# A sign-weight feed-forward and attention block on one core: layer 1's third copy of a running sum goes, its sum with the fifth product is written to that product's bank, and the queues are ordered anew

## What is computed

```python
xn = _layernorm(x, axis=-1)
# attention
q, k, v = einsum('bim,mhd->bhid', xn, wq / wk / wv);  q, k = rope(q), rope(k)
s = einsum('bhid,bhjd->bhij', q, k) / 128, masked causally
o = einsum('bhij,bhjd->bhid', softmax(s), v);  attn = einsum('bhij,hdm->bim', o, wo)
# feed-forward, w(k) = where(k, 1, -1)
h = s0 * concat([xn, -xn]) @ w(k0);  h = relu(h) * 2
h = s1 * h @ w(k1);                  h = relu(h) * 2
h = s2 * h @ w(k2)
out = x + attn + h
```

## Time and profile before

| | |
|---|---|
| median of the runs (lowest, highest) | 1728.72 us (1728.67, 1729.3) |
| the profiled execution's own time | 1728.13 us |
| its span, first to last instruction | 1726.3 us |
| PE busy / weight loads | 1713.5 us (99%) / 1202.2 us (70%) |
| ACT / DVE / POOL busy | 1467.6 (85%) / 1386.2 (80%) / 890.4 us (52%) |
| mean granted TensorE clock | 0.999 |

### The profile page before, as it was taken

How to read it: one execution, slowest core, us unless ns; L and a number is a source line. 1 busy time by engine, 2 the same in 40 slices (tenths; PEclk the granted TensorE clock), 3 DMA queues, 4 the chain that set the end, 5 groups by cost and what they waited for, 6 DMA issues and landing times.

```text
span 1726.3 us, 34270 instructions
## 1 busy us (share of the span) xinstructions
PE 1713.5 (99%) x12752; PEld 1202.2 (70%) x12752; DVE 1386.2 (80%) x3374; ACT 1467.6 (85%) x3229; POOL 890.4 (52%) x696
## 2 busy tenths in 40 slices
PE   8999999999999999999999999999999999999999
PEld 4567667677676776767667676676767767677677
DVE  8997887887878878688787877878788787886875
ACT  7898897888979889798897988979789797897984
POOL 7654655354654635556354563555635556354531
PEclk9999999999999999999999999999999999999999
DMA  5234434343434433444434343344433534353343
GB/s 177 56 72 85 93 60 93 68 90 64 76 81 65 98 60 71 86 72 83 68 62 86 74 81 68 68 85 70 92 56 82 79 61 93 58 94 71 62 81 68
DMA packets 454838, 134.08 MB, mean 78 GB/s; under 512 B 434704, under 2 KB 453648, under 8 KB 454672
## 3 DMA queue, kind: packets, MB, share of 16 engines
q1 hardware_dynamic: 454672, 131.90, 40.1%
HBM read 14.94 MB, written 8.39 MB: 14 GB/s over the span
## 4 chain that ended last, share of the span: by engine, by line
PE 95%; ACT 2%; DVE 2%; DMA 1%; SPq 0%; issue 0%; POOL 0%; DVEq 0%; ACTq 0%
PE bank L238 44%; PE bank L699 21%; PE bank L683 12%; PE bank L666 12%; PE bank L710 6%; DMA v<-in_wk 1%; ACT bank L427 1%; DVE pt L514 0%; ACT ph L431 0%; DMA xnat<-in_x 0%; DVE hb L549 0%; DVE ph L585 0%; SPq L282 0%; DVE wq L537 0%; ACT tb L409 0%
## 5 line engine op out<-in xcount | busy, mean ns | idle before, releaser
L351 POOL TENSOR_TENSOR tb<-tb,sin 128x512 f32<-128x512 f32 x256 | 324.7, 1273 | 445.4 <-ACT tb L410 442.7
L354 POOL TENSOR_TENSOR qk<-tb,qk 128x512 f16<-128x512 f32 x256 | 295.7, 1160 | 284.3 <-ACT qk L413 284.1
L699 PE MATMUL bank<-hb,wa 128*128 128x256 f16 x3360 | 391.3, 273 | 0.2 <-DVE ph L585 0.2
L699 PEld LDWEIGHTS bank<-hb,wa 128*128 128x128 fp8e5 x3360 | 327.3, 98 | 53.7 <-DVE ph L585 0.4
L427 ACT ACTIVATE bank<-bank,nm,sc 128x512 f32<-128x512 f32 (+3 forms) x512 | 301.3, 591 | 2.6
L585 DVE SCALAR_TENSOR_TENSOR ph<-bank,rk,ph 128x512 f16<-128x512 f32 (+3 forms) x512 | 254.1, 545 | 23.0 <-ACT ph L431 21.3
L575 DVE CUSTOM_DVE_ANT_0 bank<-bank,mask 128x512 f32<-128x512 f32 (+3 forms) x512 | 238.5, 518 | 20.4 <-PE bank L666 20.1
L557 DVE TENSOR_TENSOR bank<-bank,cos 128x512 f32<-128x512 f32 x256 | 176.7, 697 | 87.3 <-ACT tb L410 87.1
L683 PEld LDWEIGHTS bank<-pt,v 128*128 128x128 f16 x2304 | 203.7, 98 | 41.5 <-DMA pt<-ph 0.8
L431 ACT ACTIVATE ph<-bank,rk 128x512 f16<-128x512 f32 (+3 forms) x512 | 230.1, 541 | 2.4 <-DVE rk L582 1.4
L683 PE MATMUL bank<-pt,v 128*128 128x256 f16 (+1 forms) x2304 | 231.1, 255 | 0.0
(11 more groups left out here) (113 smaller groups left out, 2343.9 us busy)
## 6 DMA issues: line engine op xcount, KB each, us to landing
out<-xnat SPq DMA_DIRECT2D x32, 256.0 KB, 2.2
xnat<-in_x SPq DMA_DIRECT2D x15, 512.0 KB, 3.8
pt<-ph SPq DMA_TRANSPOSE x256, 4.3
o<-in_k SPq DMA_DIRECT2D x1, 1024.0 KB, 7.5
v<-in_wq SPq DMA_DIRECT2D x1, 1024.0 KB, 9.5
v<-in_wk SPq DMA_DIRECT2D x1, 1024.0 KB, 11.3
ph<-in_wv SPq DMA_DIRECT2D x1, 1024.0 KB, 13.5
o<-in_wo SPq DMA_DIRECT2D x1, 1024.0 KB, 10.9
```

What stands on the lines that cost most here:

```text
L351: pool.tensor_tensor(tb, tb, SIN[:], ALU.mult).then_inc(s_crossed, 1)
L354: pool.tensor_tensor(QK[:, g % 2, 2 * w + 1, :], TB[:, (2 * g + w) % TRING, :], QK[:, g % 2, 2 * w, :], ALU.subtract).then_inc(s_qk_lo, 1)
L699: mm = pe.matmul(ps[:, 256 * u:256 * u + 256], WA[:, w, k, (2 * j + u) * 128:(2 * j + u) * 128 + 128], HB[:, h, s, k, :], start=first and ...
```

## The change

For each j the third copy goes. `add_p5_to` reads the running sum's bank, adds S5, and writes the result into the bank of the fifth product, which `keep_p5` has read by then; product 4 accumulates on the running sum itself. The fifth product's bank is thus held until `h1_hi` and `h1_lo` have read it. The ACT queue loses 30 copies (90 to 60 instructions `bank<-bank` 128x512); every other kind of instruction keeps its count on every engine. All five orders are laid anew, from the start to the end, with another table ROTATION.

The new helper, the first line of the table, and `vector_program` in a repeated block:

```diff
+        def add_p5_to(dve, ps, dst):
+            dve.tensor_tensor(dst[:, :], ps[:, :], S5, ALU.add).then_inc(s_add, 1)
...
-            [0, 5, 1, 3, 4, 2, 6, 7],
+            [4, 6, 1, 3, 2, 0, 7, 5],
...
+                dve.wait_ge(s_prod, 14 * b - 16)
+                add_p5(dve, ps[3])
+                dve.wait_ge(s_h1_hi, 8 * b - 10)
+                h1_lo(dve, 1, 0, 1, ps[3])
+                dve.wait_ge(s_prod, 14 * b - 15)
+                add_p5_to(dve, ps[0], ps[4])
```

`scalar_program` loses the third copy there:

```diff
-                act.wait_ge(s_prod, 14 * b - 15)
-                act.wait_ge(s_rot, 16 * b - 1)
-                copy_sum(act, ps[5], ps[7])
```

At the start, `scalar_program` and then `vector_program`:

```diff
-            xT_first_hi(act, 0, BANK[0])
             xT_first_hi(act, 1, BANK[1])
-            act.wait_ge(s_k0, 2)
-            sign_k0(act, 0)
-            act.wait_ge(s_k0, 3)
-            sign_k0(act, 3)
             act.wait_ge(s_k_in[1], 16)
             convert_k1_act(act, 5)
+            xT_first_hi(act, 0, BANK[0])
...
-            dve.wait_ge(s_xT_hi, 1)
+            dve.wait_ge(s_xT_hi, 2)
             xT_first_lo(dve, 0, BANK[0])
-            dve.wait_ge(s_xT_hi, 2)
             xT_first_lo(dve, 1, BANK[1])
```

More of the change, by code:

```diff
@@ L1934, in scalar_program @@
+            h1_hi(act, 1, 1, 1, BANK[4])
+            xp_hi(act, 2)
+            act.wait_ge(s_PV, 11)
+            o_hi(act, 10, BANK[0])
             act.wait_ge(s_rot, 30)
@@ new lines, in tensor_program @@
+            pe.wait_ge(s_pt[0], 320)
+            pe.wait_ge(s_P_lo, 80)
+            values(pe, 18, BANK[6])
+            product(pe, 0, 2, range(8), BANK[5])
+            product(pe, 0, 3, range(8), BANK[3])
+            pe.wait_ge(s_o, 17)
+            qk(pe, 22, 1, BANK[2])
+            pe.wait_ge(s_rot, 43)
+            v_proj(pe, 2, 1, 3, BANK[4])
+            pe.wait_ge(s_h1, 9)
+            product(pe, 1, 5, range(8), BANK[1], first=True)
+            pe.wait_ge(s_qk_lo, 42)
+            pe.wait_ge(s_rot, 44)
@@ new lines, in tensor_program @@
+            scores(pe, 20, 0, BANK[0])
+            pe.wait_ge(s_o, 18)
+            scores(pe, 20, 1, BANK[6])
+            pe.wait_ge(s_h1, 10)
+            scores(pe, 20, 2, BANK[5])
+            pe.wait_ge(s_h1, 11)
+            product(pe, 1, 1, range(8), BANK[3], first=True)
+            pe.wait_ge(s_pt[1], 288)
+            pe.wait_ge(s_vp, 21)
+            values(pe, 17, BANK[4])
+            pe.wait_ge(s_copy, 7)
+            product(pe, 1, 2, range(8), BANK[2])
+            product(pe, 1, 6, range(8), BANK[3])
@@ new lines, in tensor_program @@
+            pe.wait_ge(s_o, 25)
+            qk(pe, 30, 1, BANK[0])
+            pe.wait_ge(s_rot, 59)
+            v_proj(pe, 3, 1, 3, BANK[5])
+            pe.wait_ge(s_h1, 17)
+            product(pe, 1, 5, range(8), BANK[4], first=True)
+            pe.wait_ge(s_qk_lo, 58)
+            pe.wait_ge(s_rot, 60)
+            scores(pe, 28, 0, BANK[7])
+            pe.wait_ge(s_o, 26)
+            scores(pe, 28, 1, BANK[2])
+            pe.wait_ge(s_h1, 18)
+            scores(pe, 28, 2, BANK[6])
@@ new lines, in tensor_program @@
+            pe.wait_ge(s_h1, 19)
+            product(pe, 1, 1, range(8), BANK[3], first=True)
+            pe.wait_ge(s_pt[1], 416)
+            pe.wait_ge(s_vp, 29)
+            values(pe, 25, BANK[5])
+            pe.wait_ge(s_copy, 11)
+            product(pe, 1, 2, range(8), BANK[0])
+            product(pe, 1, 6, range(8), BANK[3])
+            pe.wait_ge(s_o, 27)
+            qk(pe, 30, 0, BANK[5])
+            pe.wait_ge(s_P_lo, 113)
+            v_proj(pe, 3, 1, 0, BANK[7])
+            pe.wait_ge(s_P_lo, 115)
@@ new lines, in tensor_program @@
+            pe.wait_ge(s_copy, 54)
+            product(pe, 0, 7, range(8), BANK[2])
+            pe.wait_ge(s_pt[0], 1856)
+            pe.wait_ge(s_P_lo, 464)
+            values(pe, 114, BANK[4])
+            product(pe, 0, 2, range(8), BANK[1])
+            product(pe, 0, 3, range(8), BANK[3])
+            pe.wait_ge(s_o, 113)
+            qk(pe, 118, 1, BANK[5])
+            pe.wait_ge(s_rot, 235)
+            v_proj(pe, 14, 1, 3, BANK[7])
+            pe.wait_ge(s_h1, 105)
+            product(pe, 1, 5, range(8), BANK[0], first=True)
@@ new lines, in tensor_program @@
+            pe.wait_ge(s_qk_lo, 234)
+            pe.wait_ge(s_rot, 236)
+            scores(pe, 116, 0, BANK[6])
+            pe.wait_ge(s_o, 114)
+            scores(pe, 116, 1, BANK[4])
+            pe.wait_ge(s_h1, 106)
+            scores(pe, 116, 2, BANK[1])
+            pe.wait_ge(s_h1, 107)
+            product(pe, 1, 1, range(8), BANK[3], first=True)
+            pe.wait_ge(s_pt[1], 1824)
+            pe.wait_ge(s_vp, 117)
+            values(pe, 113, BANK[7])
+            pe.wait_ge(s_copy, 55)
```

6500 lines of the change are left out of this document (3194 added, 3306 removed), and 26 rows, old and new, of the table ROTATION.

## The result

The changed kernel took 1742.66 us (median of 4 runs, 1742.15 to 1743.64) beside 1728.7 us for the kernel before: a ratio of 1.0081, 95% interval 1.0063 to 1.0098. It is slower by 14 us, outside the predicted range of 1727.0 to 1733.4. Its profiled execution took 1743.64 us, with a span of 1741.8.

What follows compares the result with a forecast made beforehand. PE, at a column a cycle without idle time, was taken to bound the repeated blocks. 1728.13 + 0 (copies) + 0 (adds) + 0 (blocks) + 1.8 (start) + 0 (blocks 0 and 1) = 1729.9 us, range 1727.0 to 1733.4.

Steps and rivals of the forecast that it cites:

- The bound: Repeated blocks: PE passes a column a cycle and is never idle, so only fewer columns could make them faster.
- The copies: Dropping 30 ACT copies of 594 ns, 17.8 us of ACT's time, gives 0 because PE's work covers them.
- the rival at 1710.3: PE is not at its limit and ACT's 17.8 us come through, giving 1710.3 us; chance 0.01.
- The blocks' new orders: Reordered queues in the repeated blocks: taken as 0 us, between 0 and 4.9 us over 14 blocks.
- `o_lo`, named as the tightest: Bank 0 in the third order fence: DVE's `o_lo` ends 0.6 us before the `qk` that needs the bank.
- The slow rival: Repeated blocks: `o_lo` later than the `qk` needing its bank, 0.35 us in each of 14 blocks, 1734.8 us; chance 0.2.
- The start: Weight conversion between x's two copies delays layer 0, and the clock falls: first `qk` 1.8 us late, range 0 to 1.8.
- In both orders on the same instructions: Start, DVE from 15.33 us to the first `qk`: the same gapless work in both orders, so a 0.4 us delay stays.
- The clock rule: Start: PE idle 3.3 us before layer 0, like the 3.18 us at which the clock fell, so 1.5 us is lost.
- Blocks 0 and 1: Late matmul groups there, 1.5 us in the kernel before, could go or come again: taken as 0, range -1.5 to +1.5.

Runs made afterwards that it cites:

- e6_more_copies: e3_both with one more ACT copy into an unread spare tile ahead of each of the 30 keep_p5: 1732.76 us.
- e19_three: Changed kernel with x's two copies first, product 2 ahead of values(8b+2), and the POOL order of e15_pool_spread: 1728.40 us.
- e2_p2_first: Changed kernel with product 2 of j = 0 moved ahead of values(8b+2) on PE in blocks 2 to 14: 1732.71 us.
- e4_before_near: Kernel before with values(8b) one product later on PE in 13 blocks, leaving 6.1 us in place of 7.8 before values(8b+2): 1732.07 us.
- e1_start: Changed kernel with ACT making both copies of x before converting a part of layer 1's weights: 1740.87 us.
- e3_both: Changed kernel with x's two copies first at the start and product 2 ahead of values(8b+2): 1731.19 us.
- e9_before_late_o: Kernel before with DVE's fourth search (largest of wo) behind the three splits of wq and wk, not ahead of them: 1731.56 us.
- e12_pool_pause: Kernel before with POOL's last four sums of layer 1's weights waiting until DVE has split wq: 1730.54 us.
- e15_pool_spread: Kernel before with POOL's last four weight sums moved: two after DVE's first split of wk, two between later steps of heads 2 to 4: 1726.83 us.
- e5_load_quarter: Changed kernel with load_x of blocks 3 to 15 bringing 128 KB in place of 512, output not the reference's: 1737.10 us.

## Why the prediction was wrong

- **The bound.** "Nothing but fewer columns could make it faster", said of the repeated blocks, held. The copies were sized right at 0 in the repeated blocks (e6_more_copies, e19_three), and the rival at 1710.3 was rightly small.
- **The blocks' new orders, taken as 0, range to +4.9; they cost 9.1.** This is the step that failed. It was 9.1 us of waits for a DMA transpose at `values(8b+2)` (e2_p2_first took them away, e4_before_near made 4.0 us of them in the kernel before). The prediction took "the places where the new order leaves least between a group and the next into its bank", and looked at PSUM banks alone. `o_lo`, named as the tightest, never made PE wait. `PT` is a ring as well, of two buffers, its writer is a DMA, and behind its writer stands SP's queue, whose new order was not followed at all. The sum would have been: 6.1 us on PE against a transpose chain of some 6 us that a load can lengthen. The kernel before gave a hint: in its trace `values` waits 0.21 us once, at 1347 us, with 7.8 us of room, so in that block the slack was used up. The slow rival (chance 0.2) had the right shape, a new wait once a block, with the wrong mechanism, and 1734.8 was too low.
- **The start, +1.8; the first `qk` came 5.0 us late.** The conversion between x's copies, the idle time of PE and the falling clock were all there. Three sizes were off. Layer 1's weights landed 0.9 us later than taken, so that DVE split x from 13.04 and not from 12.3. The clock stayed low for 6.8 us, 5.6 of them in layer 0, not for "some 3 us". And so DVE waited 2.57 us for the turned maxima, not 1.45. On the time itself the conversion is worth 1.4 to 1.8 us, which is the predicted size.
- **"In both orders on the same instructions", so the rest stays.** This was wrong. Between DVE's start on the searches and the first `qk` the instructions are the same but their durations are not: `dg` took 0.55 us and now 1.03, and a split of wq took 0.8 or 2.6 us in the kernel before, 1.80 and 2.38 in the changed one, depending on what POOL did at the moment. The 3.34 us for two stood in the trace of the kernel before and was not asked about.
- **The clock rule, "the idle time is nearest to the row at which the clock fell".** An idle time of 2.0 us before layer 0 left the clock up in the kernel before and lowered it in e1_start, e3_both and e9_before_late_o. And in e2_p2_first one of 3.14 us before the first `qk` left it at 1.00, where 3.1 to 3.2 us lowered it in the kernel before and the changed one. A wait's length in one trace doesn't decide it.
- **Blocks 0 and 1, 0 within 1.5 us.** They cost 1.5 to 1.7, at the end of that range or just over it. The largest part is the 1.56 us for DVE's `rotate` at the end of block 0.

## What to carry to other kernels

When an order is laid anew, list every ring that is shared by two engines, buffers in SBUF that a DMA fills as well as PSUM banks, and for each compare the reader's distance with the writer's whole chain, its queue's issue time and the transfers ahead of it included. A repeated block whose period is the same to 0.01 us says only that the old distances sufficed; look for the smallest wait that appears once, for it can name the ring without slack, as here. And before the start of an engine's chain is taken as a sum of durations, ask of each duration that is three times its twin what stood beside it.

## What the runs showed of the hardware

DVE and POOL exclude each other in some instructions. DVE's split with both inputs in SBUF takes 0.74 to 0.75 us alone and up to 2.6 beside POOL's TENSOR_TENSOR, and then ends some 0.55 us after POOL's instruction; `dg`, a tiny instruction with SBUF inputs, took 0.23 us alone and up to 2.07 beside POOL, when it ended 0.03 us after POOL's instruction. With POOL held back, two splits of wq took 1.40 us in place of 3.34 (e12_pool_pause). Splits out of PSUM (0.68 us) and the searches with one input (2.27 us) took the same either way. The Trainium skill, in "SBUF — State Buffer", section "SBUF: two separate sides", states an exclusive lock between DVE and GpSimd that is held for the whole instruction, and that a DVE operation with two SBUF inputs takes only against a GpSimd operation that reads SBUF. The splits here agree: they have two SBUF inputs, POOL's sums read SBUF, and a split beside a sum took up to 2.6 us in place of 0.74. Keeping the two apart is what e15_pool_spread's 2.0 us rest on, the clock's part included.

A DMA transpose of `PH` to `PT` occupied SP's queue for 1.3 to 2.1 us in most places. In the changed kernel the first one issued 0.4 to 1.7 us behind the 512 KB load of x always took 2.3 to 3.6 us. Some far from any load took as long, so the load isn't the only reason; that it is one is borne out by e5_load_quarter: with a quarter of the load the same transposes took 1.3 to 3.0 us, 11 of 13 of them under 2.1, and 5 of 9 us of waits went.
